# Attention queues laid out by a table: loads issued on SyncE, normalising on GpSimd, the block copy split between VectorE and ScalarE

## The reference

```
xn  = layernorm(x)
qkv = clip(xn @ Wqkv.T, -8, 8);  q, k, v = split(qkv)
q   = layernorm(q) * q_ln_w + q_ln_b          (k likewise)
s   = (q . k) / sqrt(32) + slope[h] * (key - query), causal, 32 heads of 32
att = softmax(s) @ v @ Wout.T
ffn = xn @ binarize(Wffn).T + bias            (alpha * sign(W))
out = x + att + ffn
```

## Time and profile before

| | us |
|---|---|
| median of 3 runs | 1588.84 |
| time of the profiled execution | 1590.43 |
| its span, first to last instruction | 1588.6 |
| TensorE busy | 1430.5 (90%) |
| VectorE busy | 835.1 (53%) |
| ScalarE busy | 558.9 (35%) |
| GpSimd busy | 549.5 (35%) |
| mean granted TensorE clock | 0.964 |

### The profile page before, as it was taken

How to read it: one execution, slowest core, us unless ns; L and a number is a source line. 1 busy time by engine, 2 the same in 40 slices (tenths; PEclk the granted TensorE clock), 3 DMA queues, 4 the chain that set the end, 5 groups by cost and what they waited for, 6 DMA issues and landing times.

```text
span 1588.6 us, 24448 instructions
## 1 busy us (share of the span) xinstructions
PE 1430.5 (90%) x9256; PEld 661.4 (42%) x9256; DVE 835.1 (53%) x1310; ACT 558.9 (35%) x1049; POOL 549.5 (35%) x316
## 2 busy tenths in 40 slices
PE   4899999999999979998888888887978888889998
PEld 2455445445545434444333333333333333334443
DVE  6665354545454301266767677666666677631111
ACT  4444133323333200004554555454554555540000
POOL 4221122222222100001544555543345555565443
PEclk9999999999999989999999999999999999999999
DMA  6453232322222372211222222212222220025543
GB/s 232 154 166 112 67 78 60 79 60 69 70 73 66 90 204 80 77 57 42 69 69 64 67 69 56 52 46 63 70 69 64 67 69 24 20 82 166 159 146 119
DMA packets 145396, 136.85 MB, mean 86 GB/s; under 512 B 83744, under 2 KB 112416, under 8 KB 145120
## 3 DMA queue, kind: packets, MB, share of 16 engines
q1 hardware_dynamic: 48285, 90.80, 18.4%
q10 hardware_dynamic: 97027, 44.89, 12.0%
HBM read 93.06 MB, written 42.47 MB: 85 GB/s over the span
## 4 chain that ended last, share of the span: by engine, by line
PE 64%; issue 10%; DVE 10%; ACT 4%; DMA 4%; ACTq 3%; POOL 3%; SPq 2%; POOLq 0%; DVEq 0%
PE ps L956 39%; PE ps L1115 8%; PE ps L1031 5%; DVE arena L836 5%; PE ps L1092 5%; DVE arena L892 3%; ACT arena L672 3%; PE ps L1118 3%; PE ps L1009 2%; PE ps L1095 1%; PE ps L1034 1%; ACTq L335 1%; DMA arena<-r_scr 1%; ACTq L336 1%; DMA v_scr<-arena 1%
## 5 line engine op out<-in xcount | busy, mean ns | idle before, releaser
L956 PE MATMUL ps<-arena 128*128 128x512 f16 x3584 | 795.5, 382 | 21.6 <-DVE arena L807 11.3
L956 PEld LDWEIGHTS ps<-arena 128*128 128x128 f16 (+1 forms) x3584 | 349.8, 98 | 439.3 <-issue 13.7
L556 POOL TENSOR_TENSOR arena<-arena 128x2048 f32<-128x2048 f32 (+1 forms) x96 | 338.4, 3525 | 551.3 <-ACT arena L672 542.0
L836 DVE TENSOR_REDUCE arena<-ps 128x1 f16<-128x512 f32 (+3 forms) x768 | 382.3, 548 | 213.9 <-PE ps L1034 121.1
L672 ACT ACTIVATE arena<-ps 128x512 f32<-128x512 f32 (+3 forms) x768 | 326.9, 499 | 294.8 <-PE ps L1095 182.8
L1031 PE MATMUL ps<-arena 127*128 127x512 f16 (+3 forms) x768 | 249.4, 346 | 57.9 <-DVE arena L836 55.7
L1092 PE MATMUL ps<-arena 128*128 128x512 f16 (+3 forms) x768 | 253.0, 343 | 49.4 <-ACT arena L672 46.7
L807 DVE TENSOR_SCALAR arena<-ps 128x1024 f32<-128x1024 f32 x48 | 58.8, 1224 | 253.8 <-PE ps L956 225.0
L1115 PE MATMUL ps<-arena 128*32 128x512 f32 (+3 forms) x1536 | 163.4, 522 | 0.0
L1092 PEld LDWEIGHTS ps<-arena 128*128 128x128 f16 x768 | 77.0, 101 | 169.0 <-ACT arena L672 75.6
L1031 PEld LDWEIGHTS ps<-arena 127*128 127x128 f16 x768 | 76.9, 101 | 135.9 <-DVE arena L836 99.6
(11 more groups left out here) (50 smaller groups left out, 843.5 us busy)
## 6 DMA issues: line engine op xcount, KB each, us to landing
arena<-in_x SPq DMA_DIRECT2D x32, 512.0 KB, 4.6
arena<-in_wqkv_t SPq DMA_DIRECT2D x48, 256.0 KB, 4.0
base_scr<-arena SPq DMA_DIRECT2D x16, 512.0 KB, 2.9
q_scr<-arena ACTq DMA_DIRECT2D x16, 512.0 KB, 4.1
k_scr<-arena ACTq DMA_DIRECT2D x16, 512.0 KB, 4.4
v_scr<-arena SPq DMA_DIRECT2D x16, 512.0 KB, 2.9
arena<-r_scr SPq DMA_DIRECT2D x128, 64.0 KB, 2.0
arena<-base_scr SPq DMA_DIRECT2D x16, 512.0 KB, 3.8
```

The costliest lines, as they stand in the source:

```text
L556: nc.gpsimd.tensor_tensor(acc[:, :, at:HALF], before, p32[k % PSLOTS][:, :, 0:w], ALU.add)\
L836: ins = nc.vector.tensor_reduce(negm[s % 2][:, at:at + 1], ps[:, NATB[use(s, pos) % RB], col:col + width], AX, ALU.max, negate=True)
L956: ins = nc.tensor.matmul(dst[c], lhs(k, a), wparts[:, k, b, c * HALF:(c + 1) * HALF], start=(k == 0 and (a, b) == order[0]), stop=(k == KT ...
```

## The change

Only attention and the way into the output product are touched.

- V products are no longer issued in pairs. `PV_AFTER` says after which scores (c, j) which V product stands; -2 and -1 are chunks 10 and 11 of the group before. `NATS` says how many maxima items belong to each chunk, and `due` spreads them over its heads.
- `load_vg` and `load_stack` move from ScalarE's queue to SyncE's. The stack of group n + 2 is now loaded in group n, behind `sums_out` of the block before.
- `o_norm` and `o_low` move from VectorE to GpSimd, in one stream with the adds. That of half 0 of group n - 1 stands behind all adds of group n - 1; that of half 1 is put between the adds of group n.
- The copy out of PSUM is split: ScalarE copies O (`o_copy`, 128x512), VectorE copies S (`s_copy`, 128x512).
- `o_high` of half 0 moves from the end of group n to behind the exponentials (0, 3) of group n + 1; that of half 1 from (7, 1) to (8, 1).
- ScalarE's and VectorE's wait for the stores of V, ahead of the first exponentials, moves to the first writes that need it.
- At the end, GpSimd normalises both blocks of the last group before it prepares the residual of the output tiles. VectorE takes the last reciprocals before the first output step.

```diff
-        WORK = [span(c)[3] for c in range(NC) for j in range(GH)]
-        DUE = [ITEMS * sum(WORK[:x + 1]) // sum(WORK) for x in range(len(WORK))]
-        LAG = 2
+        NATS = [4, 3, 3, 2, 5, 4, 4, 4, 5, 4, 2, 2]
+        assert sum(NATS) == ITEMS
+
+
+        PV_AFTER = {(1, 0): [-2], (2, 0): [-1], (2, 3): [0], (4, 2): [1], (5, 2): [2], (6, 2): [3],
+                    (7, 1): [4], (8, 1): [5], (8, 3): [6], (10, 0): [7, 8], (11, 2): [9]}
+
+        def due(c, j):
+
+            return sum(NATS[:c]) + NATS[c] * (j + 1) // GH
...
-                sp.wait_ge(os_out, m + 1)
+                sp.wait_ge(s_out, m + 1)
...
+                    if n == 1:
+                        for s in range(2):
+                            sp.wait_ge(v_st[s], stored(NT // 2))
+                    if n < GROUPS - 1:
+                        load_vg(sp, n + 1)
+                    if n + 2 < GROUPS:
+                        sp.wait_ge(st_done, NC * GH * n)
+                        load_stack(sp, n + 2)
...
+            def o_norm(n, qb):
+
+                m = blk_no(n, qb)
+                pool.wait_ge(r_ld, 16 * GH * (m + 1))
+                pool.wait_ge(o_out, m + 1)
+                o = os_sb[m % 2][:, 0, :]
+                nc.gpsimd.tensor_tensor(o, o, rb[m % 2], ALU.mult).then_inc(on_done, 1)
+
+            def o_low(n, qb):
+
+                m = blk_no(n, qb)
+                pool.wait_ge(oh_done, m + 1)
+                if (n, qb) == (0, 0):
+                    for s in range(2):
+                        pool.wait_ge(v_st[s], stored(NT // 2))
+                part = [ot[n][:, s, qb * HALF:(qb + 1) * HALF] for s in range(2)]
+                nc.gpsimd.tensor_tensor(part[1], os_sb[m % 2][:, 0, :], part[0], ALU.subtract).then_inc(ol_done, 1)
...
+                    if not DIRECT[c] and CHUNKS[c][1] > 1:
+                        add_in(n, c)
+                    if n > 0:
+                        if c == 0:
+                            o_norm(n - 1, 0)
+                        if c == 2:
+                            o_low(n - 1, 0)
+                        if c == 6:
+                            o_norm(n - 1, 1)
+                        if c == 9:
+                            o_low(n - 1, 1)
+            for qb in range(2):
+                o_norm(GROUPS - 1, qb)
+                o_low(GROUPS - 1, qb)
...
-            def os_copy(n, qb):
+            def o_copy(n, qb):
 
                 m = blk_no(n, qb)
                 act.wait_ge(pv_done, n * NC + QB_END[qb] + 1)
                 need(act, ol_done, m - 1)
-                nc.scalar.activation(os_sb[m % 2], ps[:, O_BANK:O_BANK + 2, :], ACT.Copy).then_inc(os_out, 1)
+                nc.scalar.activation(os_sb[m % 2][:, 0, :], ps[:, O_BANK, :], ACT.Copy).then_inc(o_out, 1)
...
             act.wait_ge(mm_done, NT * 4)
             act.wait_ge(w_lo, ready(NT * 4 - 1))
-            for s in range(2):
-                act.wait_ge(v_st[s], stored(NT // 2))
             for n in range(GROUPS):
                 for c in range(NC):
                     for j in range(GH):
                         exps(n, c, j)
-                        if (c, j) == (2, 1) and n > 0:
-                            os_copy(n - 1, 1)
-                            if n < GROUPS - 1:
-                                load_vg(act, n + 1)
-                        if (c, j) == (7, 1) and n > 0:
-                            o_high(n - 1, 1)
-                        if (c, j) == (6, 1):
-                            os_copy(n, 0)
-                if n < GROUPS - STACKS:
-                    load_stack(act, n + STACKS)
-                o_high(n, 0)
-            os_copy(GROUPS - 1, 1)
+                        if n > 0:
+                            if (c, j) == (0, 3):
+                                o_high(n - 1, 0)
+                            if (c, j) == (2, 0):
+                                o_copy(n - 1, 1)
+                            if (c, j) == (8, 1):
+                                o_high(n - 1, 1)
+                        if (c, j) == (6, 2):
+                            o_copy(n, 0)
+            o_high(GROUPS - 1, 0)
+            o_copy(GROUPS - 1, 1)
             o_high(GROUPS - 1, 1)
...
+            def s_copy(n, qb):
 
                 m = blk_no(n, qb)
-                dve.wait_ge(r_ld, 16 * GH * (m + 1))
-                o = os_sb[m % 2][:, 0, :]
-                nc.vector.tensor_tensor(o, o, rb[m % 2], ALU.mult).then_inc(on_done, 1)
-
-            def o_low(n, qb):
-
-                m = blk_no(n, qb)
-                dve.wait_ge(oh_done, m + 1)
-                part = [ot[n][:, s, qb * HALF:(qb + 1) * HALF] for s in range(2)]
-                nc.vector.tensor_tensor(part[1], os_sb[m % 2][:, 0, :], part[0], ALU.subtract).then_inc(ol_done, 1)
-
-            dve.wait_ge(v_st[1], stored(NT // 2))
+                dve.wait_ge(pv_done, n * NC + QB_END[qb] + 1)
+                need(dve, on_done, m - 1)
+                nc.vector.tensor_copy(os_sb[m % 2][:, 1, :], ps[:, S_BANK, :]).then_inc(s_out, 1)
...
+                    if pos == due(2, 0) and n > 0:
+                        s_copy(n - 1, 1)
+                    if pos == due(6, 2):
+                        s_copy(n, 0)
+                    if pos == 16 and n > 0:
+                        recips(n - 1, 1)
                     if pos == 31:
                         recips(n, 0)
-                    if pos == 38:
-                        o_norm(n, 0)
...
-            o_low(GROUPS - 1, 0)
+            s_copy(GROUPS - 1, 1)
+            recips(GROUPS - 1, 1)
             c_out_step(0, 0)
-            recips(GROUPS - 1, 1)
-            o_norm(GROUPS - 1, 1)
-            o_low(GROUPS - 1, 1)
...
-                    need(pe, os_out, blk_no(n, qb))
+                    need(pe, o_out, blk_no(n, qb))
...
+                if first:
+                    need(pe, s_out, blk_no(n, qb))
...
-                            for pos in range(DUE[x - 1] if x else 0, DUE[x]):
+                            for pos in range(due(c, j - 1), due(c, j)):
                                 nat_item(n + 1, pos)
-                        elif x == 0:
+                        elif (c, j) == (0, 0):
                             row_b_turn(n, use(GROUPS, 0))
-                    k = n * NC + c
-                    if k % 2 and k > LAG:
-                        with_v(k - LAG - 1)
-                        with_v(k - LAG)
+                        for late in PV_AFTER.get((c, j), []):
+                            if n > 0 or late >= 0:
+                                with_v(n * NC + late)
...
-            for k in range(GROUPS * NC - LAG, GROUPS * NC):
+            for k in range(GROUPS * NC - 2, GROUPS * NC):
```

More of the change, by code:

```diff
@@ L249, in build_program @@
         pv_done = sem("pv_done")
-        os_out = sem("os_out")
+        o_out = sem("o_out")
+        s_out = sem("s_out")
         rec_done = sem("rec_done")
@@ new lines, in add_in @@
+            def add_in(n, c):
+                qb, t, at, w = span(c)
+                k = n * NC + c
+                pool.wait_ge(exp_done, GH * (k + 1))
+                if t == 2:
+                    need(pool, pv_done, n * NC)
+                need(pool, add_done, adds_for(k) - 1)
+                former = p32[(k - 1) % PSLOTS] if t == 2 else acc[:, :, at:HALF]
+                nc.gpsimd.tensor_tensor(acc[:, :, at:HALF], former, p32[k % PSLOTS][:, :, 0:w], ALU.add)\
+                  .then_inc(add_done, 1)
@@ L545, in _ @@
             for n in range(GROUPS):
                 for c in range(NC):
-                    qb, t, at, w = span(c)
-                    k = n * NC + c
-                    if DIRECT[c] or t == 1:
-                        continue
-                    pool.wait_ge(exp_done, GH * (k + 1))
-                    if t == 2:
-                        need(pool, pv_done, n * NC)
-                    need(pool, add_done, adds_for(k) - 1)
-                    before = p32[(k - 1) % PSLOTS] if t == 2 else acc[:, :, at:HALF]
@@ L556, in _ @@
-                    nc.gpsimd.tensor_tensor(acc[:, :, at:HALF], before, p32[k % PSLOTS][:, :, 0:w], ALU.add)\
-                      .then_inc(add_done, 1)
+                    if not DIRECT[c] and CHUNKS[c][1] > 1:
[9 more added lines that the diff above has]
+                            o_low(n - 1, 1)
@@ L685, in o_high @@
                 act.wait_ge(on_done, m + 1)
+                if (n, qb) == (0, 0):
+                    for s in range(2):
+                        act.wait_ge(v_st[s], stored(NT // 2))
                 nc.scalar.activation(ot[n][:, 0, qb * HALF:(qb + 1) * HALF], os_sb[m % 2][:, 0, :], ACT.Copy)\
```

12 lines of the change are left out of this document (removed).

## The result

The changed kernel took 1601.25 us (median of 9 runs, 1594.83 to 1604.64) against 1590.05 us of the kernel before beside it (1585.44 to 1593.03). The ratio is 1.007, with a 95% interval from 1.0053 to 1.0086: slower, by 11 us or 0.7%. The profiled execution has a span of 1599.5 us, 10.9 above before's 1588.6; the mean granted clock is 0.950 against 0.964.

The account below looks back on a forecast made before the run. GpSimd's chain through o_norm was to set the period, 44.7 us against 43.8. Attention +9.2, start -1.0 and end +11.2 made +19.4 on 1590.43: 1609.8, less 1.6 for the median, so 1608 us (range 1594 to 1625).

Parts of the forecast that it names:

- The gate: Attention: ScalarE's o_high of half 0 waits some 8 us for GpSimd's o_norm behind all adds, done at E + 25.6.
- E: Mark of each group in attention: the start of GpSimd's first add, when chunk 6's exponentials are done.
- From V product 11 to the next E: Rest of a period in attention: 15.1 us at full clock, plus 2.2 for the low clock after TensorE's idle.
- The first and the last period: Ends of attention: first 42.1 us, with no block before it on GpSimd; last 43.1, bound by ScalarE's exponentials.
- The way out: End of the stage: third output tile waits for residuals behind both norms on GpSimd, TensorE stands 7.9 us; +11.2 us.
- The start: First exponentials no longer wait for a store of V, but V product 0 still waits for V's load: 1 us gained.
- SyncE's burst: Seven stack issues, together 5.3 us, and V's load precede recips_in of half 1; covered by 2 to 4 us.
- Rival 3: SyncE's burst is longer than counted, o_norm of half 1 starts 2 us late each time: 1638 us, slower; chance 0.11.
- the removed loads: 13 stack loads, 5.3 us each, and 14 V loads leave ScalarE; alone up to 3 to 4 us per group.
- Rival 1: The gate is there but cheap: period 41.9 us, about 1571 us; decides from a period of 43.1 down; chance 0.18.
- Rival 2: GpSimd does not gate; TensorE's own work sets the period, some 37 us with hand-overs: about 1495 us; chance 0.04.
- Rival 4: The change does what it says and nothing follows; gate and gains cancel, within 5 us of 1589; chance 0.06.

Follow-up runs that it names:

- e1: The changed kernel with ScalarE's o_high of half 0 moved from behind exponential (0, 3) to behind (3, 3): 1539.66 us, ratio 0.9664.
- e8: The changed kernel with o_norm and o_low back on VectorE and the stack loads at the end of the group: 1529.26 us, ratio 0.9629.
- e2: The changed kernel with the residuals of output tiles 0 and 1 prepared before the last block is normalised on GpSimd: 1590.19 us, ratio 0.9981.
- e9: The changed kernel with ScalarE's wait for the stores of V put back ahead of its first exponentials: 1606.65 us, ratio 1.0091.
- e3: The changed kernel with SyncE's seven stack loads issued behind recips_in of half 1 instead of ahead of it: 1582.38 us, ratio 0.9947.
- e4: The kernel before with only the V and stack loads moved to SyncE, at the change's places: 1608.83 us, ratio 1.0089.
- e5: As e4, but the stack loads of group n + 3 stand behind recips_in of half 0, at the group's end: 1565.91 us, ratio 0.9861.
- e7: As e6, with chunk 5's sums on TensorE, so GpSimd does five adds in place of six: 1471.71 us, ratio 0.9264.
- e11: As e7, with chunk 6's sums on TensorE too, so GpSimd does four adds: 1499.6 us, ratio 0.9428.
- e6: The changed kernel with e1's and e2's edits and e5's place for the stack loads: 1508.57 us, ratio 0.9494.

## Why the prediction was right

The forecast was 1608 us and slower; it came out at 1601 and slower. By its steps:

- **The gate.** Right, and shown by e1 (62 us) and by e8. The chain from E through `o_norm` took 24.9 us against 25.6, and the wait was 7.5 us against 8. V product 11 started at E + 27.4, as forecast, but that this agrees to the tenth is luck: from `o_norm` to it took 2.5 us, at the low clock, where I had 1.75 at full clock. In four turns (758.87, 802.18, 1338.43 and 1381.83) TensorE first stood 1.9 to 3.9 us for VectorE's small subtraction, which I had put at nothing, and then less at the gate; the two periods of these that are neither the first nor the last took 44.8 and 44.7 us, so it cost nothing there, as I had argued.
- **From V product 11 to the next E.** 16.6 us in group 8 with the low clock in it, where the forecast had 15.1 + 2.2. TensorE worked for 3.8 us at 0.50, which is a loss of 1.9. Over the thirteen middle periods the mean is 44.7 us (E of group 1 at 782.76, of group 14 at 1363.25), the forecast value. That too is luck in part: one period of 46.8 (1227.04 to 1273.88) is in it, and the other twelve have a mean of 44.5.

```profile
782.76 4.55 POOL L589 TENSOR_TENSOR arena<-arena 128x2048 f32<-128x2048 f32 x1 [16.95 <-ACT arena L722]
...
1363.25 4.55 POOL L589 TENSOR_TENSOR arena<-arena 128x2048 f32<-128x2048 f32 x1 [16.96 <-ACT arena L722]
```

- **The first and the last period**: 41.5 and 41.3 against 42.1 and 43.1. I had let ScalarE bound the last one too much: 1.8 us.
- **The way out.** +10.4 against +11.2; the stall is 7.84 us against 7.9. e2 shows that it is the order on GpSimd: with the other order the end takes 184.9 us, 0.4 above before.
- **The start** is where most of the difference lies: 5.7 us gained, where the forecast had 1.0. That is 4.7 of the 8.5 us by which the span came out below the forecast's. Of this 0.9 is the projections' own scatter, 2.9 is the wait (e9), and 1.9 is the order: from first exponential to first add 17.7 us against 19.6. The step that failed is "V product 0 still waits for V's load": SyncE waits only for the stores of the first sequence before that load and issued it at 723.41, so V had landed, and V product 0 (728.34) waited for nothing.
- **SyncE's burst.** The margin of 2 to 4 us was too generous: `o_norm` of half 1 waited in 11 places within attention, 0.3 to 2.2 us each and 9.8 in all; the other 7.6 us of the 17.4 are at the way out. Rival 3's mechanism is thus real but small here, and e3's 19 us are more than these waits. In the text on the removed loads I priced them "alone" at 3 to 4 us per group; e4 shows that in the changed place they cost 16 us instead, and e5's place gives 23.
- **Rival 1** (a cheap gate) failed at its condition, a period below 43.1. **Rival 2** was right in that TensorE's own work allows some 37 us, which e7 reached at 36.5, but that took a shorter chain on GpSimd, a small subtraction clear of the adds, and the gate moved. **Rival 4** (within 5 us) fails by the 11 us measured.

## What to carry to other kernels

When work moves to an engine that was idle, look at who waits for the end of its queue and not at its load: GpSimd was busy for 25 us of 44 here, and one consumer behind its last operation set the period. When a chain is cut, look at where the small operations of other engines fall against the large ones that remain: e7 and e11 differ by that above all. An in-order consumer of a late result belongs as late in its own stream as its buffers allow. A burst of large loads goes where no small, awaited transfer is issued behind it on the same queue.

## What was not expected of the hardware

An 8 KB store issued on SyncE behind 2 MB of loads on the same queue took 5.6 us until the next step could start (e4: 915.50 plus 0.58, to 921.69). With no load ahead of it the kernel before shows 1.1 us (1047.56 plus 0.38, to 1049.02), on SyncE in group 7:

```profile
1046.80 0.52 SPq L408 DMA_DIRECT2D arena<-arena  x1
1047.56 0.38 SPq L425 DMA_DIRECT2D r_scr<-arena  x1
1049.02 1.72 SPq L429 DMA_DIRECT2D arena<-r_scr  x4
```

A VectorE subtraction of 128x16 with two SBUF operands took 0.39 us in e7 and 3.32 beside a GpSimd add of 128x1536 in e6 (medians of 16), where it ended with the add.

After 7.42 us of standing TensorE had 0.50 for 3.8 us more, and after 3.79 us in the earlier trace rows for 5.99 more. The difference is in how much of the low level fell into the standing, where it costs nothing: the mean granted clock was 0.82 over the 7.43 us, which is 2.7 us at 0.50, and 0.89 over the 3.79, which is 0.8. So the length of a wait alone did not tell what it costs in clock.
